# Layer 1 of an attention and expert kernel: TensorE's product with the values moved behind the transposes of the stacks

## What is computed

```python
x = x + conv_attention(group_norm(x))   # layer 0: shifted 8x8 windows, 12 heads of 8
t = tokens(x)
# layer 1: 6 heads of 16, causal, a band of 16 keys back, one sequence of 256 per image
qkv = layer_norm(t) @ qkv_w + qkv_b
att = where(causal & (|i - j| <= 16), q @ k.T / 4, -inf)
t = t + (softmax(att) @ v * gate) @ proj_w + proj_b
# experts: 4 experts of 96 -> 384 -> 96 with gelu, the best 2 of each token
t = t + experts(layer_norm(t))
```

## Time and profile before

| | |
|---|---|
| median of 3 runs | 501.06 us (499.53 to 501.89) |
| the profiled execution | 497.59 us, of which 493.5 us are the span of the trace |
| layer 1's steps 1 to 31 in the span | about 219 to 332 us |
| busy in the span | PE 88%, DVE 73%, ACT 68%, POOL 27% |

### The profile page before, as it was taken

One profiled execution on the slowest core, in us unless ns is written; L12 is line 12 of the kernel. 1 busy time (PEld: TensorE's weight loads), 2 busy tenths in 40 slices (PEclk: granted clock), 3 DMA queues, 4 the chain that ended last, 5 costly groups with the idle time before them and its releaser, 6 DMA issues.

```text
span 493.5 us, 14736 instructions
## 1 busy us (share of the span) xinstructions
PE 433.9 (88%) x5354; PEld 324.2 (66%) x5354; DVE 362.0 (73%) x1056; ACT 335.1 (68%) x898; POOL 131.6 (27%) x257
## 2 busy tenths in 40 slices
PE   2547999999999996889999999788998999999995
PEld 1114767777776765667777777566885677777773
DVE  4976778787888788457767777647677777777776
ACT  1016787777778785268888888555777777777773
POOL 8302222222121226033433334553912000000000
PEclk9999999999999999589999999997999999999998
DMA  7112000000000000000000000000500232212300
GB/s 174 23 30 71 28 8 0 0 0 1 0 0 0 0 0 2 1 2 3 3 0 0 0 0 0 2 1 1 129 2 17 68 81 80 57 25 80 80 14 18
DMA packets 14326, 12.36 MB, mean 25 GB/s; under 512 B 12803, under 2 KB 13143, under 8 KB 13528
## 3 DMA queue, kind: packets, MB, share of 16 engines
q1 hardware_dynamic: 13128, 11.74, 9.3%
q10 hardware_dynamic: 1072, 0.08, 0.2%
q0 software_dynamic: 96, 0.14, 0.1%
HBM read 10.31 MB, written 1.70 MB: 24 GB/s over the span
## 4 chain that ended last, share of the span: by engine, by line
PE 65%; ACT 10%; DVE 10%; SPq 6%; issue 4%; DMA 2%; POOL 1%; DVEq 0%; ACTq 0%
PE bank L651 8%; PE bank L663 6%; PE score_banks L718 5%; PE score_banks L1283 4%; PE score_banks L1280 4%; PE score_banks L1281 4%; PE bank L684 3%; PE bank L708 3%; PE bank L590 3%; PE score_banks L1269 3%; PE score_banks L625 3%; PE score_banks L1270 3%; ACT probsT L816 3%; PE score_banks L1271 3%; PE score_banks L606 2%
## 5 line engine op out<-in xcount | busy, mean ns | idle before, releaser
L985 POOL TENSOR_TENSOR stack<-qk,ones 128x192 f16<-128x192 f32 x64 | 32.4, 506 | 183.2 <-DVE qk L907 115.4
L1432 DVE TENSOR_TENSOR hidden_lo<-hidden,hidden_hi 128x512 fp32r<-128x512 f32 x96 | 65.6, 685 | 20.1 <-ACT hidden_hi L1336 20.0
L839 DVE TENSOR_REDUCE negmax<-score_banks 128x12 bf16<-128x768 f32 (+1 forms) x64 | 48.2, 754 | 25.7 <-PE score_banks L625 25.7
L651 PEld LDWEIGHTS bank<-vals,probsT 128*64 128x64 f32 (+1 forms) x1536 | 36.9, 127 | 29.0 <-ACT probsT L813 19.1
L651 PE MATMUL bank<-vals,probsT 128*64 128x18 f32 (+1 forms) x1536 | 42.5, 208 | 13.9 <-ACT probsT L816 4.5
L1334 ACT ACTIVATE hidden<-score_banks 128x512 f32<-128x512 f32 x64 | 38.3, 598 | 21.7 <-PE score_banks L1271 17.7
L718 PE MATMUL score_banks<-perm,probs 128*128 128x128 f32 x288 | 43.9, 281 | 0.7 <-ACT probs L786 0.7
L663 PE MATMUL bank<-w_qkv,xnT 128*128 128x192 f32 x128 | 40.2, 398 | 3.9 <-DVE qk L907 3.0
L1280 PE MATMUL score_banks<-hidden_hi,w_hi 128*96 128x512 f32 x96 | 38.6, 402 | 2.2 <-ACT hidden_hi L1336 2.2
L1283 PE MATMUL score_banks<-hidden_lo,w_hi 128*96 128x512 f32 x96 | 38.5, 401 | 1.7 <-DVE hidden_lo L1432 1.7
L813 ACT ACTIVATE probsT<-score_banks 128x384 f32<-128x384 f32 x32 | 15.7, 490 | 34.4 <-PE score_banks L718 34.4
(11 more groups left out here) (195 smaller groups left out, 1105.5 us busy)
## 6 DMA issues: line engine op xcount, KB each, us to landing
xT_all<-gate_scratch SPq DMA_DIRECT2D x8, 768.0 KB, 5.2
x_all<-in_x SPq DMA_DIRECT2D x4, 384.0 KB, 7.3
out<-moe_final SPq DMA_DIRECT2D x8, 192.0 KB, 2.2
w<-in_w SPq DMA_DIRECT2D x1, 582.0 KB
w<-in_w SPq DMA_DIRECT2D x1, 576.0 KB
bias_f<-col_scratch SPq DMA_DIRECT2D x16, 24.0 KB
perm<-in_permutations SPq DMA_DIRECT2D x1, 320.0 KB, 3.2
w_qkv<-in_w_qkv SPq DMA_DIRECT2D x2, 109.1 KB
```

The source lines that it names most:

```text
L651: last = pe.matmul(o_bank[rows, pair_of[h2] * 2 * vd:(pair_of[h2] + 1) * 2 * vd], probsT[:, h2, rows], buffer_of(k, odd, -1)[:, w, pair_of ...
L839: v.tensor_reduce(negmax[:].rearrange("p (g h) -> p g h", g=2), score_banks[k][:, :, 0:half].rearrange("p g (h j) -> p g h j", j=KEYS), AX ...
L1432: v.tensor_tensor(hidden_lo[m % HBUF][:], hidden[m % 2][:], hidden_hi[m % HBUF][:], ALU.subtract).then_inc(q["hidden_lo"], 1)
```

## The change

In `pe_step`, in the branch for layer 1, the call of `pe_values` moves from directly behind `pe_scores` to behind `pe_stacks`. Its waits move with it. No instruction is added or removed, and no other engine's order changes.

```diff
@@ -736,10 +736,10 @@
             pe_shift(pe, n, k)
             pe_values(pe, n, b, k, odd)
             return
-        pe_values(pe, n, b, k, odd)
         pe_project_qk(pe, n, b, k, xnT)
         pe_shift(pe, n, k)
         pe_stacks(pe, n)
+        pe_values(pe, n, b, k, odd)
         pe_project_v(pe, n + 2, k, xnT)
```

## The result

The changed kernel took 511.94 us (median of 4 runs, 509.75 to 514.2), the kernel before 500.29 (498.73 to 501.89, with one more run than shown above). These two medians are 11.65 us apart, 2.3%. The ratio on record, which is the figure for the change, is **1.0306** (95% interval 1.0252 to 1.036); it implies some 496.7 us for the kernel before, and 3.06% of 501.06 are 15.3 us. The four runs of before do not show that baseline, but a second study of the same two kernels on one chip bears it out: 509.28 against 495.35 us, 1.030 (1.0251 to 1.035). So the change is slower, as forecast, by 14 to 15 us in place of 9.1. The median of 511.94 lies close to the forecast of 510, but that is luck of the baseline, which stood higher in those few runs.

What follows compares the result with a forecast made beforehand. The prediction took PE as the bound. Middle pairs 7.3, step 1 0.3 and steps 29 to 31 1.5 sum to 9.1 us, added to the shown median: 510.1, rounded to 510; range 504.5 to 514.0.

Steps and rivals of the forecast that it cites:

- The wait for the copy goes: Layer 1: PE's wait for ACT's copy of transposed probabilities vanishes; with small waits around it, at most 0.76 us per pair.
- The shift loses its cover, 0.36 us per step: Layer 1's shift waits for the maximum; PE fills 0.69 of 1.05 us, idling 0.36 per step, 0.72 per pair.
- The division comes late and DVE's queue with it: Even steps: output transposes wait 0.24 us for the division; DVE's queue delays the next maximum, idling PE 0.30 more.
- Rival B: DVE's queue does not bind; only the shift's 0.36 per step and the 0.24 stay: about +4.5, 505.6; chance 0.17.
- The pair of 7.40 us: Steps 2 to 28: a pair lasts 7.40 us against 6.86, 0.54 more; 13.5 pairs make 7.3 us.
- Steps 29 to 31 cost 1.5 us, 2.0 at most: Layer 1's last three steps cost 1.5 us, bounds 0.7 and 2.0; step 30's later wait swallows most of its cost.
- The clock, no term: Layer 1: gaps of 0.3 to 0.6 us don't lower PE's clock, so the sum holds no term for it.
- Rival D: The clock falls: a quarter of the pairs at the lower level would cost 21 us more, 531; chance 0.04.
- Rivals C and E: C: maximum ready when PE reaches the shift, 496, chance 0.04; E: gains and losses cancel within 2.5 us, chance 0.06.
- A: The forecast itself: shift and DVE's queue both bind in layer 1; +7.5 to +11 us, chance 0.66.
- slower end than the bounds allow: Layer 1's last steps cost more than the bounds of 0.7 and 2.0 us; the remaining chance, 0.03.

Runs made afterwards that it cites:

- first experiment: Against the kernel before: product with the values behind the query and key projection, ahead of the shift; 491.37 against 496.76 us, 0.9909.
- second experiment: Against the changed kernel: DVE's statistics and two copies ahead of the division in even steps; 507.24 us, 1.0223 against the kernel before.
- e4: Against the changed kernel: product with the values back in its old place in steps 29 to 31; 505.49 us, 1.0165 against the kernel before.
- best version: Against the kernel before: first experiment's order plus constant transposes in layer 0's step 30 and layer 1's step 29; 487.34 against 495.35 us, 0.9827.
- a1: The changed kernel timed again, against the kernel before on one chip; 509.28 against 495.35 us, 1.030.
- e2: The second experiment: against the changed kernel, DVE's statistics ahead of the division; 507.24 us, 1.0223 against the kernel before.
- e5: Against the kernel before: product with the values in its new place only in steps 29 to 31; 500.35 against 495.35 us, 1.0099.
- e7: Against the changed kernel: 22 constant transposes fill PE's wait in step 29; 509.38 us, 1.0263 against the kernel before.
- e10: Against the kernel before: only steps 29 to 31 moved, constant transposes filling waits in steps 29 and 30; 497.59 against 496.93 us, 1.0028.

## Why the prediction was wrong, point by point

The direction, the mechanism and the place of each wait in the middle were right; the size was not. The range's top was 514.0, 2.6% above 501.06, and the change is 3.06%. Two terms of the sum were too small: the pair (7.40 us, measured 7.60) and the last three steps (1.5 us, measured 5.0 to 6.4); and the clock, which had no term, is a part of the second.

- **The wait for the copy goes:** right. No row of it is left.
- **The shift loses its cover, 0.36 us per step:** right. The shift comes 1.05 behind the scores in the step with the odd product (267.90 to 268.95). PE's own work fills 0.65 of it and not 0.69, because the scores take 0.22 until the projection and not 0.26, so it idles 0.40. The first experiment, which keeps the cover, turns +15 into -4.5 us.
- **The division comes late and DVE's queue with it:** right in kind. The queue held the shift 0.25 us per pair, forecast 0.30, by the second experiment. Rival B, in which it does not bind, is refuted.
- **The pair of 7.40 us:** the first term that failed. It is 7.60, so 0.74 and not 0.54 us are lost, and 13.5 pairs of 0.20 are 2.7 us. I took the slots of the old order for the new one. From shift to product it is 0.60 or 0.61, not 0.50 or 0.52, in both steps (0.19 in all). The value projection takes 0.53 behind the product, not 0.47 behind the stacks, and the output projection 0.49, not 0.42, in the odd step, where the latter also starts 0.07 later than walked; that DVE's way in the even step is 0.10 shorter than walked (V + 3.16 for 3.26) offsets a part. The weight loads point to a reason for some of it. In the value projection they start with the first product (269.88 for both), where they were 0.06 ahead (268.57 for 268.63); in the output projection the first weight load starts 0.04 ahead of the first product (266.79 for 266.83), where it was 0.11 (269.21 for 269.32). The Trainium skill ("TensorE: Matmul & The Clock Gate", section "Step-by-step: what each phase is for") says that weight loads are pulled ahead of products in flight. The rows agree, and the slots are longer by just what the lead is shorter, 0.06 and 0.07; no run tried it apart. The other 0.1 of each step went with the moved product: 24 small products start some 0.1 later than another group would, behind the scores as well (0.29 against 0.22), and the walk left that in the scores' slot when it moved them behind the stacks. Why they do wasn't tried either.
- **Steps 29 to 31 cost 1.5 us, 2.0 at most:** the term that failed most. They cost 5.0 measured alone (3.3 to 6.5 by the interval of the ratio), and 6.4 in the profiled execution. Two parts were mis-sized. In the steps themselves, the walk had step 30 swallow most of its cost in a later wait, where 0.54 us more lie between its shift and the next, and gave step 31 0.7, where it takes 0.89 (both from the kernel with only steps 30 and 31 moved). And the clock stayed low longer. Of the ends measured (labels cut to their first part; for the kernel with the value projection ahead of the shift no end was formed):

| steps 29 to 31 | end, us | of it at the lower clock |
|---|---|---|
| old place: before, e4 | 32.28, 33.56 | 10.2, 17.0 |
| ahead of the shift: first experiment, best version (filled) | 32.16, 33.01 | 10.2, 17.1 |
| product between shift and stacks | 36.11 | 20.5 |
| new place, no fill: a1, e2, e5, changed kernel | 35.99, 36.38, 38.79, 38.72 | 17.1, 20.5, 27.3, 30.7 |
| new place, filled: e7, e10 | 34.77, 35.19 | 13.7, 17.1 |
| new place in 29 only, in 30 and 31 only | 35.00, 36.73 | 20.5, 23.9 |

At about 17 us of lower clock, 35.99 stands against 33.0 to 33.6: by this estimate the places themselves are some 2.5 us. Two profiles of the same changed kernel differ by 2.7 us (38.72 less 35.99) for 13.6 us more at the lower clock, 0.2 us for each; the 20.5 us more that the changed kernel's profile has than that of the kernel before then make the other 4. These are single executions.
- **The clock, no term:** right for the middle, where the digits stay 9 with a wait in every step, wrong for the end. The prediction also misread: the digit 7 stands for 333 to 345 us, which is not the long wait before step 29's shift (319.42) but the beginning of the expert stage. The kernel before has a low stretch at both places:

```profile
313.00:323.00 10.00, 6.74 (x90) 5.88 (x91) 5.37 (x23) 4.54 (x14) 6.26 (x7) 0.83 0.01 2
323.00:332.00 9.00, 6.63 (x142) 4.95 (x140) 5.07 (x17) 6.26 (x15) 5.39 (x8) 1.00 0.01 2
332.00:344.00 12.00, 9.78 (x59) 7.35 (x59) 7.31 (x36) 5.89 (x11) 3.36 (x4) 0.72 0.00 0
```

In the first profile of the changed kernel the clock does not come back between the two. Rival D had the mechanism, but for the middle. The Trainium skill's rule on frequent small idle times (same page, section "A second HAM failure mode: psum-queue depth-cycling") does not hold in the rows of the middle, with PE busy 13.44 of 15 us. The last steps, where the waits stand at 0.6 to 0.8 us, fit it better, but no row settles it: the best version runs 196 to 214 us at the full clock with PE busy only 12.29 of 18 us, and the kernel with the value projection ahead of the shift, with waits of up to 0.8 us in 24 steps of the middle, is at the full clock there but for some 3 us near 272 us.
- **Rivals C and E:** neither. Nothing in the changed kernel starts a maximum sooner. What came is A with a pair too short, and the "slower end than the bounds allow" that had a chance of 0.03.

## What to carry to other kernels

Before moving a product to escape one wait, list what its old place covered: the time from a result to the next instruction that needs it (here 1.05 us from scores to shift) must be filled by what stays between. Often the best place is not the far one but the first that is late enough: here the product moved behind one group (0.43 us) gained 0.9%, and moved behind three (0.93 us) it lost 3.0%. Where a pipeline drains, steps have less to hide waits behind, so price them apart from the steady state, and with the clock in mind.

## What the runs showed of the hardware that was not expected

- The time at TensorE's lower clock differs between runs of the same kernel by up to 21 us (18.7 to 39.7), and the run's time by up to 8 us (493.4 to 501.2). The two go together only loosely: the run of 501.15 us had 27.9 us of it.
- With constant transposes in a wait of 3.3 us the clock stayed at 1.00 over 18 us where it is 0.53 in the kernel before. At the end of layer 1 the same made no clear difference in one kernel (1.0263 against 1.030, intervals overlapping); in another the ratio is 1.0028 with fills and 1.0099 without, on two chips.
- A group's slot depends on its neighbours: 0.33 us from the stacks to the value projection but 0.43 to the 24 small products, and 0.47 for the value projection behind the stacks but 0.53 behind those products.
